# Graph-network kernel: part of the by-source sums moved from their own stage into the scatter stage

## The chip, the cores and the metric

One NeuronCore of one Trainium2 chip runs the whole kernel in one launch. The metric is device time in microseconds (us). The clock of TensorE that the throttle granted is recorded beside the instructions.

## The reference

There are 3125 nodes with 128 features and 53125 directed edges (`src`, `dst`, sorted by `dst`, self-loops included) with 128 features each. Four residual layers follow one another, each on `relu(layernorm(x))`:

```
h = relu(layernorm(x))
L0: agg = sum of edge_attr over edges by src + by dst;  x += relu([h, agg] @ W1 + b1) @ W2 + b2
L1: agg = sum of edge_attr over edges by dst;           x += relu([h, agg] @ W1 + b1) @ W2 + b2
L2: two graph convolutions with D^-1/2 A D^-1/2
L3: messages relu([h[src], h[dst], edge_attr] @ W) @ W2 + b, mean by dst, update MLP
```

The change concerns the sum of edge rows by `src` that L0 needs. Everything after the first two stages below stays as it is, but for small things named with the change.

## The kernel before

Edges come in 416 chunks of 128, two chunks make a pair (208 pairs), four chunks or two pairs make a group (104 groups). Nodes come in 25 blocks of 128.

**Scatter stage** (`place_and_count`, from 26 to 557 us). For each pair the engines do this. SyncE (SP) loads a group's edge rows into one of 8 buffers. VectorE (DVE) makes one-hots of the pair's blocks and of its window of 24 destinations (`hots`, L814 and L821). ScalarE (ACT) makes one-hots of the low part of the source (`lows`, L786 and L789) and copies the source key into the edge rows (`key_in_row`, L779). TensorE (PE) multiplies them into PSUM (L921 for a table of counts between nodes, L927 for the sums by destination, L930 for counts by destination). DVE adds the pair's result to the tables in SBUF (`collect`, L853 and L855); in the order of the code, `collect(i - 2)` comes behind `hots(i)`.

Once a group, PE computes ranks of the edges within their source blocks (`rank`, L901, L892, L905), DVE turns them into a row number of the table `rows_by_block` in DRAM (`own_rank` L834, `place` L839, `place_whole` L843), and GpSimd (POOL) writes the group's rows there with four indirect DMAs (L769). `which_block` (L828) makes the one-hots that a later `rank` needs; in group g it waits for `rank(g + 1)`, since they share two buffers. A `value_load` of the window's first column stands ahead of each `collect`. ACT copies the running counts to SBUF (`base_of_next`, L793).

The order on PE within a group g, with the even pair i = 2g and the odd pair i + 1, is: three matmuls of ones (L384, into a bank that nobody reads; 16 instead of 3 ahead of every 32nd pair), `rank(g + 1)`, the even pair, three matmuls of ones, the odd pair. The order on DVE is: even step: `place`, `hots`, `place_whole`, `which_block(g + 2)`, `collect`; odd step: `hots`, `collect`, `own_rank(g + 1)`.

**Sum stage** (`sum_blocks`, from 559 to 686 us). `rows_by_block` holds for each block of source nodes room for 18 tiles of 128 rows (9 for the last block). SP reads it in 74 reads of up to 6 tiles into 4 buffers, a read waiting for the sums of the fourth before it. DVE compares the keys with an iota (L1125), PE multiplies rows by the one-hots (L1181, a float32 product is recorded as two matmuls), and DVE adds the sum of each block to the sums by destination (L1117). Beside it DVE takes the statistics of x (L1068, L1147), and ACT checks 25 stripes of the table of counts for overflow (L1164). A short block with the flags and twelve matmuls of ones follows (L1201 to L1225), and then the dense layers.

Of the kernel before, what the change touches and what calls it, by code (L numbers as in the profile page):

```python
# [81 lines left out]
LAST_BANK = 7  # L82
WARM_EVERY = 32


class Signal:
# [6 lines left out]
    def __init__(self, make, everywhere=False):  # L93
        self.make, self.everywhere, self.on_path, self.base = make, everywhere, {}, {}

    @property
    def h(self):
        branch = Signal.path is not None and not self.everywhere
        if branch not in self.on_path:
            self.on_path[branch] = self.make()  # L100
        return self.on_path[branch]
# [44 lines left out]
def build(nc, x, src, dst, ea, l0, l1, l2, l3, out):  # L146
    ctx = ExitStack()
    with ctx:
# [7 lines left out]
        def signal(name, everywhere=False):  # L156
# [3 lines left out]
            return Signal(make, everywhere)  # L160
# [98 lines left out]
        bounds = sb("bounds", [1, 2, NB])  # L259
        over = sb("over", [1, 2, NB])  # L260
# [22 lines left out]
        tab_row = sb("tab_row", [1, 2, 2, ST * P], I32)  # L283
        tab_bc = sb("tab_bc", [P, 2, 2, ST * P])

        shifts = [sb(f"shift{k}", [P, SLOTS_OF[k], GS[k]]) for k in range(2)]
# [15 lines left out]
        junk = grid_space.take([P, NP], U8)  # L302
        excess = grid_space.take([P, NB])
# [349 lines left out]
        pair_done = signal("pair_done")  # L653
        taken = signal("taken")
# [68 lines left out]
        def place_and_count():  # L723
# [15 lines left out]
            with nc.Block(no_gpsimd_drain=True) as block:  # L739
                @on(block.sync)  # L740
                def _(sp):
                    for g in range(ROWG, GROUPS):
# [6 lines left out]
                        if g == 6 * ROWG:  # L749
                            sp.wait_ge(vec.h, vec.at(1))  # L750
                            sp.dma_start(x_nm[:, 0:NB - 1, :], x[0:(NB - 1) * P, :].rearrange("(b p) f -> p b f", p=P)).then_inc(loaded.h, 16)
                            sp.dma_start(x_nm[0:NLAST, NB - 1, :], x[(NB - 1) * P:N, :]).then_inc(loaded.h, 16)
                    sp.wait_ge(loaded.h, loaded.at(16 * 23))
# [19 lines left out]
                def _(act):  # L773
# [16 lines left out]

                    def base_of_next(g):
                        act.wait_ge(ranks_read.h, ranks_read.at(g + 1))
                        act.activation(bases[:, (g + 1) % 2, :], acc[0:1, R_AT + RANKS:R_AT + RANKS + NK], ACT.Copy).then_inc(based.h, 1)  # L793
# [4 lines left out]
                    for i in range(PAIRS):  # L798
# [4 lines left out]
                        if i % PG == 1 and g + 1 < GROUPS:  # L803
                            base_of_next(g + 1)

                @on(block.vector)
                def _(dve):
# [50 lines left out]

                    which_block(0)
                    which_block(1)  # L860
                    own_rank(0)
                    for i in range(PAIRS + 2):
# [9 lines left out]
                        if i >= 2:  # L872
                            collect(i - 2)
                        if i % PG == 1 and g + 1 < GROUPS:
                            own_rank(g + 1)
                        if i == 4 * ROWG * PG:
                            dve.wait_ge(tail_zero.h, tail_zero.at(32))
                            dve.memset(x_nm[:, NB - 1, :], 0.0).then_inc(vec.h, 1)
                    dve.memset(odd[:, 3:5], 0.0)
                    dve.tensor_scalar(bounds[:, 0, 0:NB - 1], iota[0:1, 0:NB - 1], float(CAP), float(FILLED), ALU.mult, ALU.add)  # L880
# [6 lines left out]
                    dve.tensor_tensor(over[:, 1, :], bases[:, GROUPS % 2, 0:NB], bounds[:, 1, :], ALU.is_gt)  # L887

                @on(block.tensor)
                def _(pe):  # L890
# [1827 lines left out]
```

## Time and profile before

| what | value |
|---|---|
| median of the runs shown | 1446.84 us (1445.10 to 1453.07, 3 runs) |
| the profiled execution, its own time | 1445.09 us |
| its span, first to last instruction | 1443.2 us |
| mean granted clock of TensorE | 0.971 of full |
| busy share PE / DVE / ACT / POOL | 86% / 61% / 38% / 56% |

A busy share is an average over stages. In a timeline row the first number is the start in us from the span's start, the second how long the row lasts, then engine, line, operation, and tiles as out<-in. Brackets give idle time of the engine ahead of the row and what ended it. A time of a matmul includes the way through the array, so the start of the next one tells better how long it holds the engine.

### The profile page before, as it was taken

What the parts mean: (1) busy time and instruction counts of PE and PEld (TensorE: products, weight loads), DVE (VectorE), ACT (ScalarE), POOL (GpSimd) and SP (SyncE); (2) the same over time, 40 slices, a digit from 0 to 9 for tenths busy, and PEclk for the clock granted to TensorE, in tenths of its full rate; (3) what the DMA queues carried; (4) which work ended last, traced back from release to release, by engine and by line L of the source; (5) the groups of instructions that cost most, each with busy time, mean ns of one, the idle gap of its engine ahead of it and who ended that gap; (6) DMA issues with size and microseconds to landing.
All of it is one profiled execution on the core that took longest, in us unless ns stands there. A gap on an engine that the chain in (4) does not pass through costs nothing. (4 is left out here: it accounts for less than half of the span.)

```text
span 1443.2 us, 32570 instructions
## 1 busy us (share of the span) xinstructions
PE 1243.0 (86%) x9643; PEld 908.2 (63%) x9644; DVE 881.1 (61%) x2785; ACT 555.4 (38%) x1465; POOL 809.5 (56%) x844
## 2 busy tenths in 40 slices
PE   5887888888888887898679998999999988898896
PEld 3554555555555555888459997477766766666665
DVE  6777878787877876766676537344444444444343
ACT  5444444444454446960222103333332222222222
POOL 5777777777777773000000000777777777777774
PEclk9999999999999999999889998899999999999997
DMA  7533335333333324877600001745555565555641
GB/s 230 137 106 104 104 105 148 102 105 104 106 104 106 107 72 138 237 246 217 30 18 2 2 1 52 203 133 153 156 154 155 161 159 150 152 140 145 149 111 42
DMA packets 198603, 174.73 MB, mean 121 GB/s; under 512 B 48820, under 2 KB 171174, under 8 KB 198342
## 3 DMA queue, kind: packets, MB, share of 16 engines
q1 hardware_dynamic: 171848, 118.36, 31.1%
q0 software_dynamic: 26624, 54.79, 12.9%
q8 instruction: 62, 1.02, 0.3%
q14 instruction: 69, 0.57, 0.2%
HBM read 134.89 MB, written 38.16 MB: 120 GB/s over the span
## 5 line engine op out<-in xcount | busy, mean ns | idle before, releaser
L2192 POOL DMA_INDIRECT between<-p_table,src_g x416 | 397.5, 956 | 472.5 <-DMA p_table<-n_nm 346.0
L384 PE MATMUL acc<-ones_b 128*128 128x512 bf16 x1603 | 425.5, 386 | 29.3 <-PEq L1407 15.5
L769 POOL DMA_INDIRECT rows_by_block<-h_t,mean_bc x312 | 300.6, 963 | 109.5 <-issue 77.1
L384 PEld LDWEIGHTS acc<-ones_b 128*128 128x128 bf16 x1603 | 142.5, 99 | 130.9 <-issue 39.2
L921 PE MATMUL acc<-n_nm 128*128 128x384 bf16 (+1 forms) x832 | 140.8, 291 | 87.2 <-DVE n_nm L821 86.4
L2302 ACT ACTIVATE between<-acc 128x256 f32<-128x256 f32 x208 | 79.9, 384 | 352.4 <-PE acc L2359 339.3
L853 DVE TENSOR_TENSOR between<-between,acc 128x600 f32 x208 | 161.3, 775 | 61.3 <-issue 51.7
L2391 PE MATMUL acc<-w_msg,between 128*128 128x128 f32 x832 | 184.1, 303 | 0.0
L2370 PEld LDWEIGHTS acc<-between 128*128 128x128 f32 x832 | 128.9, 197 | 71.4 <-issue 52.2
L2229 DVE TENSOR_TENSOR between<-acc,between 128x256 f32<-128x256 f32 x208 | 87.6, 421 | 139.9 <-DMA between<-p_table,src_g 90.0
L921 PEld LDWEIGHTS acc<-n_nm 128*128 128x128 bf16 x832 | 66.3, 97 | 164.0 <-DVE n_nm L821 134.8
L2370 PE MATMUL acc<-between 128*128 128x24 f32 x832 | 132.5, 240 | 42.4 <-DVE agg_sum L2269 40.7
L821 DVE TENSOR_SCALAR n_nm<-iota_w,agg_sum 128x600 bf16<-128x600 f16 x416 | 154.5, 412 | 0.0
L786 ACT ACTIVATE away<-iota_b,agg_sum 128x128 bf16<-128x128 bf16 x416 | 140.9, 385 | 0.0
L2391 PEld LDWEIGHTS acc<-w_msg,between 128*128 128x128 f32 x832 | 126.0, 191 | 1.7 <-issue 0.3
L793 ACT ACTIVATE bases<-acc 1x26 f32<-1x26 f32 x104 | 19.0, 182 | 265.7 <-DVE agg_sum L834 265.7
L1181 PE MATMUL acc<-n_nm,h_t 128*128 128x128 f32 x882 | 109.4, 280 | 11.5 <-DVE n_nm L1125 10.9
L769 POOL DMA_INDIRECT rows_by_block<-agg_sum,mean_bc x104 | 99.7, 959 | 32.5 <-issue 25.5
L2359 PE MATMUL acc<-ident,between 128*128 128x128 f32 x416 | 114.1, 275 | 0.0
L1181 PEld LDWEIGHTS acc<-n_nm,h_t 128*128 128x128 f32 x882 | 102.2, 191 | 18.8 <-DVE n_nm L1125 18.1
L789 ACT ACTIVATE n_nm<-away,ones 128x256 bf16<-128x256 bf16 x208 | 105.6, 508 | 6.8
L2269 DVE TENSOR_TENSOR agg_sum<-agg_sum,acc 128x24 f32 x208 | 37.4, 180 | 115.3 <-PE acc L2370 65.5
(204 smaller groups left out, 1950.4 us busy)
## 6 DMA issues: line engine op xcount, KB each, us to landing
h_t<-rows_by_block SPq DMA_DIRECT2D x73, 387.0 KB, 3.8
between<-in_edge_attr SPq DMA_DIRECT2D x207, 128.0 KB
h_t<-in_edge_attr SPq DMA_DIRECT2D x78, 256.0 KB, 3.2
between<-in_dst SPq DMA_DIRECT2D x51, 288.0 KB
between<-p_table,src_g POOLq DMA_INDIRECT x416
agg_sum<-in_edge_attr SPq DMA_DIRECT2D x25, 256.0 KB
rows_by_block<-h_t,mean_bc POOLq DMA_INDIRECT x312
rows_by_block<-x_nm SPq DMA_DIRECT2D x1, 4644.0 KB, 18.6
```

The lines of the kernel that those rows point to most:

```text
L384: pe.matmul(acc[:, bank * BANK:(bank + 1) * BANK].rearrange("p (a n) -> p a n", n=P), ones_b[:, :], ones_b[:, :].rearrange("p (a n) -> p a ...
L769: pool.indirect_dma_start(rows_by_block, bass.IndirectOffsetOnAxis(ap=place_in_table[:, t:t + 1], axis=0), row_group(g)[:, j, :], None).th ...
L786: act.activation(away[:, h + j, :], iota_b[:, :], ACT.Abs, scale=-1.0, bias=lo_s[:, 2 * i + j:2 * i + j + 1])\
L789: act.activation(low_hot[:, h:h + 2, :], away[:, h:h + 2, :], ACT.Relu, scale=-1.0, bias=ones[:, 0:1]).then_inc(lows_made.h, 1)
L821: ins = dve.tensor_scalar(wide_hot[:, i % HOTB * 2 + j, :], iota_w[:, :], key_w[:, t:t + 1], None, ALU.is_equal)
L853: dve.tensor_tensor(between[:, :, bass.ds(first, W)], between[:, :, bass.ds(first, W)], acc[:, o:o + NB * WS].rearrange("p (b w) -> p b w" ...
L921: pe.matmul(acc[:, to:to + (b1 - b0) * WS].rearrange("p (b w) -> p b w", w=WS)[:, :, 0:W], low_hot[:, h + j, :], wide_hot[:, h + j, b0 * W ...
L1181: last = pe.matmul(acc[:, o:o + P], rows_in_block[:, q, j, 0:D], hot_in_block[:, q, j, :], start=is_first and j == 0, stop=is_last and j = ...
L2192: pool.indirect_dma_start(got[:, q, j * D:(j + 1) * D], None, p_table, bass.IndirectOffsetOnAxis(ap=src_g[:, n * G + j:n * G + j + 1], axi ...
L2359: last = pe.transpose(acc[:, o:o + P], rows[:, i, j, :], ident[:, :])
L2370: last = pe.matmul(acc[:, o:o + W], relued[:, i % MR, j, :], onehot[:, i * G + j, :], start=j == 0, stop=j == G - 1)
L2391: last = pe.matmul(acc[:, o:o + P], turned[:, i % MR, j * P:(j + 1) * P], w_msg[:, 2, :], start=False, stop=True)
```

## The change

Seventy-two chunks of 384 rows of `rows_by_block`, that is the first nine tiles of each of the 24 full blocks, are summed within the scatter stage. SP loads chunk m in its step of group m + 32 (three buffers; it waits for the sum three chunks before). ACT makes the one-hots in group m + 29: three operations of Abs and one of Relu, both float32. PE sums the chunk in group m + 30, ahead of the odd pair, in place of the three matmuls of ones there: three float32 products into the one idle bank. DVE takes it out in group m + 31 into a new table `home`, behind `collect` of the odd step. As there is one bank, `sum_chunk(m)` waits for `take_chunk(m - 1)`. `rank` moves ahead of the ones of the even pair. The wait for `taken` moves ahead of the ones too, which now go to the pair's own bank. The 16 ones come ahead of an even pair.

In the sum stage each full block has nine tiles left, as reads of 6 and 3; 50 reads in all. The load of x moves from the scatter stage to behind the fifth read. ACT checks 14 stripes alone, and the other 11 as one that DVE unites with ten bitwise ors of 800 words (r = 5 to 14). DVE adds `agg_dst` to `home` once (3072 columns), statistics come two to a read from read 16 on. The 16 ones at its start become 6, the 12 ones of the flags' block go, and the first dense layer gets three. Three comparisons with bounds come at the end of the scatter stage, and some semaphores of the general path are shared with others.

```diff
+CT = 3
+CROWS = CT * P
+CRING, CHOTS = 3, 3
+CHUNK_LOAD, CHUNK_HOT, CHUNK_SUM, CHUNK_TAKE = 32, 29, 30, 31
+CHUNKS = EC // KC - CHUNK_LOAD
...
 @on(block.sync)
+                    def load_chunk(m):
+                        if m >= CRING:
+                            sp.wait_ge(chunk_summed.h, chunk_summed.at(m + 1 - CRING))
+                        row = m % (NB - 1) * CAP + m // (NB - 1) * CROWS
+                        sp.dma_start(chunk_rows[:, m % CRING, :, :], rows_by_block[row:row + CROWS, :].rearrange("(p j) w -> p j w", j=CT))\
+                          .then_inc(chunk_in[m % CRING].h, 16)
...
+                        if g >= CHUNK_LOAD:
+                            load_chunk(g - CHUNK_LOAD)
...
 @on(block.scalar)
+                    def hots_of_chunk(m):
+                        act.wait_ge(chunk_in[m % CRING].h, chunk_in[m % CRING].at(16 * (m // CRING + 1)))
+                        if m >= CHOTS:
+                            act.wait_ge(chunk_summed.h, chunk_summed.at(m + 1 - CHOTS))
+                        h = chunk_hot[:, m % CHOTS, :, :]
+                        for j in range(CT):
+                            act.activation(h[:, j, :], iota[:, :], ACT.Abs, scale=-1.0, bias=chunk_rows[:, m % CRING, j, D:KW]).then_inc(chunk_away.h, 1)
+                        act.wait_ge(chunk_away.h, chunk_away.at(CT * (m + 1)))
+                        act.activation(h, h, ACT.Relu, scale=-1.0, bias=ones[:, 0:1]).then_inc(chunk_hots.h, 1)
...
+                        if i % PG == 0 and 0 <= g - CHUNK_HOT < CHUNKS:
+                            hots_of_chunk(g - CHUNK_HOT)
...
 @on(block.vector)
+                    def take_chunk(m):
+                        dve.wait_ge(chunk_summed.h, chunk_summed.at(m + 1))
+                        at = home[:, m % (NB - 1) * P:m % (NB - 1) * P + P]
+                        o = IDLE_BANK * BANK
+                        if m < NB - 1:
+                            dve.tensor_copy(at, acc[:, o:o + P]).then_inc(chunk_taken.h, 1)
+                        else:
+                            dve.wait_ge(chunk_taken.h, chunk_taken.at(m + 2 - NB))
+                            dve.tensor_tensor(at, at, acc[:, o:o + P], ALU.add).then_inc(chunk_taken.h, 1)
...
                         if i >= 2:
                             collect(i - 2)
+                        if i % PG == 1 and 0 <= g - CHUNK_TAKE < CHUNKS:
+                            take_chunk(g - CHUNK_TAKE)
                         if i % PG == 1 and g + 1 < GROUPS:
                             own_rank(g + 1)
...
 @on(block.tensor)
+                    def sum_chunk(m):
+                        pe.wait_ge(chunk_hots.h, chunk_hots.at(m + 1))
+                        if m >= 1:
+                            pe.wait_ge(chunk_taken.h, chunk_taken.at(m))
+                        o = IDLE_BANK * BANK
+                        for j in range(CT):
+                            last = pe.matmul(acc[:, o:o + P], chunk_rows[:, m % CRING, j, 0:D], chunk_hot[:, m % CHOTS, j, :],
+                                             start=j == 0, stop=j == CT - 1)
+                        last.then_inc(chunk_summed.h, 1)
...
                     for i in range(PAIRS):
                         g, q, c = i // PG, i // PG % ROWG, i % PG * 2
-                        stream_ones(pe, IDLE_BANK, WARM_UP if i % WARM_EVERY == WARM_EVERY - 1 else WARM_PAIR)
                         if c == 0 and g + 1 < GROUPS:
                             rank(g + 1)
+                        if i >= PRING:
+                            pe.wait_ge(taken.h, taken.at(i + 1 - PRING))
+                        if c != 0 and 0 <= g - CHUNK_SUM < CHUNKS:
+                            sum_chunk(g - CHUNK_SUM)
+                        else:
+                            stream_ones(pe, at_bank(i) // BANK, WARM_UP if i % WARM_EVERY == WARM_EVERY - 2 else WARM_PAIR)
                         pe.wait_ge(hots_made.h, hots_made.at(i + 1))
                         pe.wait_ge(lows_made.h, lows_made.at(i + 1))
-                        if i >= PRING:
-                            pe.wait_ge(taken.h, taken.at(i + 1 - PRING))
...
 sum_blocks
-                for j in range(0, n, LR):
+                done = CT * sum(b < k for k in BY_CHUNK)
+                for j in range(done, n, LR):
...
+                        if r == LB_IN:
+                            sp.wait_ge(vec.h, vec.at(1))
+                            sp.dma_start(x_nm[:, 0:NB - 1, :], x[0:(NB - 1) * P, :].rearrange("(b p) f -> p b f", p=P)).then_inc(loaded.h, 16)
...
-                        dve.tensor_tensor(agg_sum[:, b * P:b * P + P], acc[:, o:o + P], agg_dst[:, b * P:b * P + P], ALU.add).then_inc(agg_read.h, 1)
+                        dve.tensor_tensor(agg_sum[:, b * P:b * P + P], acc[:, o:o + P], home[:, b * P:b * P + P], ALU.add).then_inc(agg_read.h, 1)
...
-                    stream_ones(pe, LAST_BANK, WARM_UP)
+                    stream_ones(pe, LAST_BANK, WARM_SHORT // 2)
```

## Rows read from the trace of the kernel before

**Rows 1.** The profile page, its first line.
```profile
span 1443.2 us, 32570 instructions
```

**Rows 2.** Windows over both stages: busy us of each engine, PEclk, DMA share, GB/s.
```profile
562.30:684.20 121.90, 110.58 (x884) 102.06 (x883) 80.92 (x147) 74.58 (x49) 0.00 (x0) 0.99 0.77 235
26.00:557.30 531.30, 439.81 (x3491) 273.49 (x3489) 416.17 (x1297) 253.75 (x824) 400.32 (x416) 1.00 0.37 106
```

**Rows 3.** Timeline of POOL, first DMAs of two groups.
```profile
305.25 0.96 POOL L769 DMA_INDIRECT rows_by_block<-agg_sum,mean_bc  x1 [0.30 <-ACT h_t L779]
...
310.30 0.96 POOL L769 DMA_INDIRECT rows_by_block<-agg_sum,mean_bc  x1 [0.30 <-ACT h_t L779]
```

**Rows 4.** Timeline of DVE over one group of the scatter stage.
```profile
304.00 0.65 DVE L821 TENSOR_SCALAR n_nm<-iota_w,agg_sum 128x600 bf16<-128x600 f16 x2
...
305.37 0.27 DVE L828 TENSOR_TENSOR agg_sum<-iota,agg_sum 128x104 bf16<-128x104 f32 x1 [0.46 <-PE acc L905]
306.19 0.78 DVE L853 TENSOR_TENSOR between<-between,acc 128x600 f32 x1 [0.55 <-issue]
...
307.00 0.87 DVE L821 TENSOR_SCALAR n_nm<-iota_w,agg_sum 128x600 bf16<-128x600 f16 x2
307.79 0.77 DVE L853 TENSOR_TENSOR between<-between,acc 128x600 f32 x1
...
308.59 0.25 DVE L834 TENSOR_TENSOR agg_sum<-acc,agg_sum 128x104 f32<-128x104 f32 x1
...
310.43 0.27 DVE L828 TENSOR_TENSOR agg_sum<-iota,agg_sum 128x104 bf16<-128x104 f32 x1 [0.24 <-PE acc L905]
```

**Rows 5.** Timeline of PE over the same group.
```profile
307.92 0.69 PE L921 MATMUL acc<-n_nm 128*128 128x384 bf16 x4 [0.95 <-DVE n_nm L821]
...
308.88 0.81 PE L384 MATMUL acc<-ones_b 128*128 128x512 bf16 x3
309.62 0.48 PE L901 MATMUL acc<-bases,ones 1*128 1x130 f32 x2
...
310.28 0.67 PE L921 MATMUL acc<-n_nm 128*128 128x384 bf16 x4
```

**Rows 6.** Groups of instructions by line: busy us, mean ns | idle before them.
```profile
L1125 DVE TENSOR_TENSOR n_nm<-iota,h_t 128x768 f32<-128x768 f32 x73 | 69.9, 957 | 40.4 <-DMA h_t<-rows_by_block 39.5
L1125 DVE TENSOR_TENSOR n_nm<-iota,h_t 128x384 f32<-128x384 f32 x1 | 0.6, 558 | 1.3 <-DMA h_t<-rows_by_block 1.3
L1117 DVE TENSOR_TENSOR agg_sum<-acc,by_dst 128x128 f32<-128x128 f32 x25 | 6.6, 269 | 0.0
L786 ACT ACTIVATE away<-iota_b,agg_sum 128x128 bf16<-128x128 bf16 x416 | 140.9, 385 | 0.0
```

**Rows 7.** Timeline of PE: the first sums, and the ones of the flags' block.
```profile
564.88 7.19 PE L1181 MATMUL acc<-n_nm,h_t 128*128 128x128 f32 x60
...
687.95 2.75 PE L384 MATMUL acc<-ones_b 128*128 128x512 bf16 x12
```

**Rows 8.** Windows in the message stage, columns as in rows 2.
```profile
1274.00:1280.00 6.00, 4.12 (x33) 3.04 (x32) 1.50 (x6) 1.13 (x4) 4.48 (x6) 1.00 0.73 170
1281.00:1283.00 2.00, 2.00 (x12) 1.82 (x11) 1.54 (x6) 0.26 (x1) 1.64 (x2) 0.50 0.48 140
...
1418.00:1424.00 6.00, 3.35 (x30) 2.84 (x28) 1.54 (x5) 1.76 (x5) 4.48 (x6) 0.99 0.27 77
...
1075.00:1081.00 6.00, 4.52 (x38) 3.40 (x36) 2.57 (x8) 1.38 (x5) 4.66 (x5) 1.00 0.53 153
```

**Rows 9.** Timeline of PE: pauses ahead of those windows, and four ones at either clock.
```profile
1278.87 0.37 PE L2370 MATMUL acc<-between 128*128 128x24 f32 x2 [1.88 <-DVE agg_sum L2269]
...
593.68 2.50 PE L1181 MATMUL acc<-n_nm,h_t 128*128 128x128 f32 x20 [1.70 <-DVE n_nm L1125]
...
1205.80 1.91 PE L384 MATMUL acc<-ones_b 128*128 128x512 bf16 x4
1209.31 1.03 PE L384 MATMUL acc<-ones_b 128*128 128x512 bf16 x4
```

More of the change, by code:

```diff
@@ L154, in build, with signal @@
         made_signals = [0]
-        def signal(name, everywhere=False):
+        def signal(name, twin=None, everywhere=False):
             def make():
@@ L258, in build @@
         bases = sb("bases", [1, 2, NK])
-        bounds = sb("bounds", [1, 2, NB])
-        over = sb("over", [1, 2, NB])
+        chunk_space = Space(x_nm[:, :, :].rearrange("p b f -> p (b f)")[:, (CAP - FILLED) // P * KW if FILLED else 6 * KW:], F32)
+        chunk_rows = chunk_space.take([P, CRING, CT, KW])
+        chunk_hot = chunk_space.take([P, CHOTS, CT, P])
+        bounds = chunk_space.take([1, 2 + len(BY_CHUNK), NB])
+        over = chunk_space.take([1, 2 + len(BY_CHUNK), NB])
+        counts_at = chunk_space.take([1, len(BY_CHUNK), NB])
         low_bound = sb("low_bound", [P, 1])
@@ L280, in build @@
         b1_row = sb("b1_row", [P, H2])
-        tab_row = sb("tab_row", [1, 2, 2, ST * P], I32)
-        tab_bc = sb("tab_bc", [P, 2, 2, ST * P])
-        shifts = [sb(f"shift{k}", [P, SLOTS_OF[k], GS[k]]) for k in range(2)]
+        home = sb("home", [P, NP])
+        general_space = Space(home[:, :], F32)
+        tab_row = general_space.take([1, 2, 2, ST * P], I32)
+        tab_bc = general_space.take([P, 2, 2, ST * P])
+        shifts = [general_space.take([P, SLOTS_OF[k], GS[k]]) for k in range(2)]
         win_f = sb("win_f", [1, PAIRS])
@@ L653, in build @@
         pair_done = signal("pair_done")
+        chunk_in = [signal(f"chunk_in{q}") for q in range(CRING)]
+        chunk_away = signal("chunk_away")
+        chunk_hots = signal("chunk_hots")
+        chunk_summed = signal("chunk_summed")
+        chunk_taken = signal("chunk_taken")
         taken = signal("taken")
@@ L887, in _ @@
                     dve.tensor_tensor(over[:, 1, :], bases[:, GROUPS % 2, 0:NB], bounds[:, 1, :], ALU.is_gt)
+                    for c, n in enumerate(BY_CHUNK):
+                        dve.tensor_tensor(over[:, 2 + c, 0:n], counts_at[:, c, 0:n], bounds[:, 2 + c, 0:n], ALU.is_lt)
                 @on(block.tensor)
@@ L941, in place_and_count @@
             away_made.passed(EC)
-            loaded.passed(16 * 23)
+            for s in (chunk_hots, chunk_summed, chunk_taken):
+                s.passed(CHUNKS)
+            chunk_away.passed(CT * CHUNKS)
+            for q in range(CRING):
+                chunk_in[q].passed(16 * len(range(q, CHUNKS, CRING)))
+            loaded.passed(16 * 21)
             vec.passed(2)
@@ L1162, in _ @@
                 def _(act):
-                    for b in range(NB):
-                        act.activation(junk[:, :], between[:, b, :], ACT.Relu, bias=low_bound[:, :], accum_out=excess[:, b:b + 1]).then_inc(checked.h, 1)
-                        if b < NB - 1:
+                    for b in range(ALONE + 1):
+                        if b == ALONE:
+                            act.wait_ge(united.h, united.at(NB - ALONE - 1))
+                        of = between[:, b, :] if b < ALONE else mean_bc[:, 2 * EC:2 * EC + NP // 4].bitcast(U8)
+                        act.activation(junk[:, :], of, ACT.Relu, bias=low_bound[:, :], accum_out=excess[:, b:b + 1]).then_inc(checked.h, 1)
+                        if b < ALONE:
                             act.wait_ge(checked.h, checked.at(b + 1))
@@ L1188, in sum_blocks @@
             agg_read.passed(NB)
-            checked.passed(NB)
+            homes.passed(1)
+            far_read.passed(1)
+            loaded.passed(32)
+            checked.passed(ALONE + 1)
+            united.passed(NB - ALONE - 1)
             vec.passed(4)
```

93 lines of the change are left out of this document (61 added, 32 removed).

## The prediction

> **What bounds the kernel now.** I read the page's span, then windows over the two stages, then one group of the scatter stage on each engine in the timeline, then groups by line. The scatter stage is 531 of 1443 us; no engine fills it: PE is busy 440 us, DVE 416, POOL 400, at full clock throughout [rows 1, 2]. POOL issues its four DMAs of a group in 5.06 us without a pause beyond 0.30 [rows 3]. DVE's group takes the same 5.06 us, from one `which_block` (L828) to the next [rows 4].
>
> That match hides a second bound, a circle between DVE and PE, which the rows show as starts that hang on each other: L828 at 305.37, the even `collect` 306.19, odd `hots` 307.00 to 307.87, the odd pair on PE 307.92, ones 308.88, `rank` 309.62, L828 again 310.43 [rows 4, 5]. L828 waits for `rank`, `rank` stands behind the odd pair in PE's order, and the odd pair waits for `hots`. There is no slack in it but what POOL adds: two L821 in a row take 0.65 us beside no hold-up and 0.87 us in the odd step [rows 4], so the circle alone would take some 4.84 us and is held at POOL's pace.
>
> The sum stage is bound by its reads: 441 tiles of 66 KB (128 x 129 x 4 bytes) are 29.1 MB in 121.9 us, while DVE is busy 81 us and waits 40 us for reads [rows 2, 6]. PE is nearly full there, 111 us [rows 2].
>
> **Scatter stage, groups with a chunk.** The sums go where ones stood, and DVE's operation is short, but the place decides. `sum_chunk(m)` runs in group m + 30 ahead of the odd pair, and waits for `take_chunk(m - 1)`. That one runs in group (m - 1) + 31, the same group, on DVE behind the odd `collect`. So the odd pair, which waited for odd `hots` alone, now waits for `collect`, the take and the sum as well. Behind it on PE stand `rank` and, through it, L828. The new circle, from L828:
> - to where a take can start, that is where L834 starts now: 308.59 - 305.37 = 3.22 us, less 0.22 us where POOL does not hold the two L821: 3.00 [rows 4];
> - the take, like L1117 (128x128 out of PSUM): 0.27 us [rows 6]; 0.05 us to PE (307.87 to 307.92 now);
> - the sum: three float32 products are six recorded matmuls, 7.19 / 60 = 0.12 us each [rows 7]: 0.72 us;
> - the odd pair, 308.88 - 307.92 = 0.96 us; then `rank`: 310.43 - 309.62 = 0.81 us and 0.10 us ahead of it. The ones between (0.64 us) are gone from here, since `rank` moved ahead of them [rows 5].
>
> Sum: 3.00 + 0.27 + 0.05 + 0.72 + 0.96 + 0.91 = 5.91 us. I take 5.95, for a rest of POOL's hold-ups; ends 5.85 and 6.15 (all of the 0.22 stays). Against 5.06 that is 0.89 us more in 71 groups (31 to 101; the first sum waits for no take): **+63 us** at full clock.
>
> The clock may not stay. In the new circle PE does ones and the even pair until 1.6 us past L828 (0.64 + 0.96), and then waits until 3.3: a pause of 1.7 us in every 5.95 us. It is busy 4.25 us of 5.95, 72%; today its pause is 0.95 us [rows 5]. In the message stage a pause of 1.88 us, in six microseconds with PE busy 4.12, was followed by the lower of the two levels, 1.2 instead of 2.4 GHz; another fall followed six microseconds at 3.35. None followed six at 4.52, nor the single pause of 1.70 us in the sum stage [rows 8, 9]. Six microseconds of the new circle have 4.3, close to the first case; and here the pause returns each time, beside pairs whose L927 and L930 stream only 24 columns. I take it that the clock falls again and again. At half clock four ones take 1.91 us instead of 1.03 [rows 9], a doubling of what lies between starts; PE's 0.72 + 0.96 + 0.81 double, so the circle is 5.95 + 2.4 = 8.3 us. In that state PE has hardly a pause left, so the clock should come back, as it came back between 1205.8 and 1209.3 us, with PE at work throughout [rows 9]. With a third of the time at half clock the mean is 1 / (0.667 / 5.95 + 0.333 / 8.3) = 6.57 us: 1.51 x 71 = **+107 us**. A fifth of the time gives 6.31 (+89), three quarters 7.56 (+177).
>
> The Trainium skill (TensorE: Matmul & The Clock Gate, HAM oscillation) describes loops whose matmuls wait in every step and which fall to the lower clock in each; by it the state would recur as I take it, and this trace shows only single falls.
>
> **Groups without a chunk** (1 to 29). With `rank` ahead of the ones the circle is 4.84 - 0.64 = 4.2 us, and DVE's own work some 4.3. POOL still needs 5.06, but has eight buffers to fall behind in, and DVE's lead is kept as the later circle is slower than POOL. What DVE can gain is bounded by 0.75 x 29 = 22 us, and by nothing if POOL holds its L821 and casts at its own pace, as it does now. I take 0.3 us each, **-9 us**.
>
> For the low end there is a rule: The Trainium skill (SBUF — State Buffer, Who interferes with whom) calls the port pair of DVE and GpSimd an exclusive lock, in which the second to start waits for the whole instruction. By it this term would be near 0. The stretched L821 [rows 4] agrees in kind, but the stretch is 0.22 us, less than a DMA of 0.96.
>
> **Covered parts.** ACT: three Abs at no more than 0.385 [rows 6] and a Relu, about 1.6 us a group ahead of the odd `lows`, on an engine busy 254 of 531 us [rows 2]; those lows end some 1.7 us past L828, PE wants them at 4.0. SP: the chunk's load is issued after a sum, two circles ahead of ACT's need, some 7 us, and its wait delays the next group's load to five groups ahead of its use: nothing. 14 MB more traffic at a DMA share of 0.37: nothing. If a load lands late, ACT holds the odd pair; about 2 us of slack go first. POOL now waits for DVE, so its last group ends sooner: -1. The 16 ones move to where PE has its pause: nothing.
>
> **Sum stage.** 225 tiles are left, 14.9 MB, and x adds 1.6: at 235 GB/s 70 us. DVE: 80.9 - 70.5 + 25 x 0.957 + 25 x 0.558 + ten unions of 800 words (0.957 x 800 / 768 = 1.0 each) + 3072 columns of `home` (0.957 x 4 = 3.8) = 62 us. PE: 450 x 0.12 = 54 us. With three engines this close, six ones instead of 16 at a cold start, and x in the way of reads, I take 74 us instead of 122: **-48**, ends -52 and -40. ACT has 14 checks instead of 25 and ends earlier than that. Flags' block: the ones (2.75 us) ended it: **-2**, ends -3 and 0, since a colder clock follows.
>
> **Sum.** The profiled execution took 1445.1 us, 1.7 below the median of the runs. Fixed terms: -9 - 1 - 48 - 2 = -60. With the falling clock 1445.1 - 60 + 107 = 1492; against the median **1494 us**. Its own range, by 89 and 177, is 1475 to 1564.
>
> **The rivals.**
> 1. The clock holds. Then +63 meets -60: 1445.1 + 3 + 1.7 = 1450. By the ends (+56, -22, -52, -3, -3 against +77, 0, -40, 0, 0) 1423 to 1484. For: single pauses of 1.7 us passed, and 75% busy passed [rows 8, 9].
> 2. Faster: the circle isn't one, since POOL sets the pace. It has this for it that DVE idles over 1 us in each group and PE 0.95 [rows 4, 5], room for a take of 0.27 and 0.08 more on PE. The scatter stage stays at its length: 1446.8 - 1 - 48 - 2 = 1396. It decides from the point where the take could reach PE without delaying `rank` by over 0.2 us; the orders written in the code speak against it.
> 3. At half clock for most of the 71 groups: 3.2 x 71 = 230, 1617. Against it: full work brings the clock back.
>
> **Chances.** Forecast with a falling clock 0.60, rival 3 0.04, rival 1 0.24, rival 2 0.12. A change under 0.5% (7 us) can't be told from none in this kernel. Rival 1 lies on both sides: faster 0.06, within 0.5% 0.10, slower 0.08. So faster 0.18, same 0.10, slower 0.72. The range of 8 in 10 leaves out rival 2, rival 3 and the lowest part of rival 1: 1432 to 1565.
>
> **What would show it.** Scatter stage: L828 to L828 near 5.9 us or more from group 31 on, PE idle 1.7 us ahead of the sum, ended by DVE's take; POOL pausing for L843; PEclk below 1.00 in windows there. Before group 31, periods under 5.06. The reads of the sum stage within 70 to 82 us. Wrong, if the period with chunks stays near 5.06, if PE's sum waits for nothing, or if the clock stays at 1.00 (then 1450).

## The result, and the profile after

The changed kernel takes **1515.84 us** (median of 4 runs, 1509.24 to 1525.08); the kernel before, run beside it, 1446.32 (4 runs, 1445.1 to 1453.07). The ratio is 1.0493, with an interval of 1.0463 to 1.0522: slower. The profiled execution took 1509.24 us. On four of the five occasions on which the experiments below ran (e1 to e7, e11 and e12), every kernel, the one before too, took about 1,800 to 1,880 us, with stops of some 3 to 9 us in which DVE waits for nothing that the profile names, so from those runs only the groups without a stop, called quiet, are read, and their times and ratios (which leave out each kernel's slowest runs) decide nothing.

The page's first line and the clock's row of the changed kernel, in 40 slices of the span:

```profile
span 1507.4 us, 32653 instructions
...
PEclk9999878878887788689999999779999999999996
```

Windows over the changed kernel: groups 1 to 26 or so, groups 33 to 101, the sum stage (columns: length; busy us of PE, PEld, DVE, ACT, POOL; PEclk, DMA share, GB/s):

```profile
26.00:158.00 132.00, 121.72 (x970) 82.79 (x969) 108.04 (x357) 70.75 (x232) 99.97 (x104) 0.99 0.41 114
170.70:649.70 479.00, 390.71 (x2576) 291.67 (x2574) 282.09 (x943) 275.89 (x840) 281.57 (x292) 0.79 0.38 107
672.30:754.60 82.30, 61.27 (x450) 55.96 (x450) 60.26 (x144) 43.20 (x31) 0.00 (x0) 0.94 0.64 191
```

These answer to [rows 1, 2]. The clock, 1.00 through the whole scatter stage before, is 0.79 in the groups with a chunk and stays at 0.99 in those without. The sum stage moves 191 GB/s instead of 235, the rate in rows 2.

How long a group takes is read from the starts of `which_block` (L828 before, L870 after; one a group, two groups ahead). First the kernel before, then the changed one: the start that opens group 1, the one that ends group 29, the one that opens group 31, the last.

```profile
25.15 0.27 DVE L828 TENSOR_TENSOR agg_sum<-iota,agg_sum 128x104 bf16<-128x104 f32 x1
...
172.18 0.27 DVE L828 TENSOR_TENSOR agg_sum<-iota,agg_sum 128x104 bf16<-128x104 f32 x1 [0.37 <-PE acc L905]
177.04 0.27 DVE L828 TENSOR_TENSOR agg_sum<-iota,agg_sum 128x104 bf16<-128x104 f32 x1 [0.18 <-PE acc L905]
...
541.31 0.27 DVE L828 TENSOR_TENSOR agg_sum<-iota,agg_sum 128x104 bf16<-128x104 f32 x1 [0.46 <-PE acc L905]
```

```profile
25.63 0.27 DVE L870 TENSOR_TENSOR agg_sum<-iota,agg_sum 128x104 bf16<-128x104 f32 x1
...
158.17 0.27 DVE L870 TENSOR_TENSOR agg_sum<-iota,agg_sum 128x104 bf16<-128x104 f32 x1
163.34 0.27 DVE L870 TENSOR_TENSOR agg_sum<-iota,agg_sum 128x104 bf16<-128x104 f32 x1 [0.68 <-PE acc L964]
...
649.71 0.27 DVE L870 TENSOR_TENSOR agg_sum<-iota,agg_sum 128x104 bf16<-128x104 f32 x1 [1.44 <-PE acc L964]
```

So groups 1 to 29 went from 147.03 us to 132.54, **-14.5**, and groups 31 to 101 from 364.27 to 486.37, **+122.1**: 5.13 against 6.85 us a group. Five of these 71 groups hold the sixteen ones: at full clock they take 6.74 us before and 6.78 after, and the others mostly 5.05 and 6.00. Fourteen groups before took 4.82 to 4.86, which is the circle alone, 4.84, of the prediction. What DVE waits for ahead of that line, over the whole kernel (us, times), before and after:

```profile
  PE acc L905: 47.2, 99
```

```profile
  PE acc L964: 164.6, 84
```

That is 117 us more of waiting for `rank`. The rest of the span: the first one-hot of the sum stage to the last add went from 123.8 us (562.3 to 686.1) to 82.3 (672.3 to 754.6), **-41.5**; from there to the first dense center 5.5 to 3.1, **-2.4**; between the last `which_block` and the first one-hot 21.0 to 22.6, +1.6; start +0.5; all behind the sums 751.6 to 749.7, -1.9. With group 30 (+0.3) these make +64.2 us, the difference of the spans (1507.4 - 1443.2).

Now one group of the changed kernel, PE and then DVE. It begins at half clock and ends at full clock:

```profile
301.94 1.40 PE L972 MATMUL acc<-x_nm 128*128 128x128 f32 x6 [1.88 <-DVE home L906]
303.13 1.21 PE L993 MATMUL acc<-n_nm 128*128 128x384 bf16 x4
...
309.73 0.91 PE L972 MATMUL acc<-x_nm 128*128 128x128 f32 x6 [0.50 <-DVE home L906]
310.47 0.67 PE L993 MATMUL acc<-n_nm 128*128 128x384 bf16 x4
...
311.49 0.48 PE L960 MATMUL acc<-bases,ones 1*128 1x130 f32 x2
...
315.72 1.52 PE L972 MATMUL acc<-x_nm 128*128 128x128 f32 x6 [1.88 <-DVE home L906]
```

```profile
306.28 0.27 DVE L870 TENSOR_TENSOR agg_sum<-iota,agg_sum 128x104 bf16<-128x104 f32 x1 [3.18 <-PE acc L964]
...
308.50 0.77 DVE L895 TENSOR_TENSOR between<-between,acc 128x600 f32 x1
...
309.31 0.27 DVE L906 COPY home<-acc 128x128 f32<-128x128 f32 x1
...
312.31 0.27 DVE L870 TENSOR_TENSOR agg_sum<-iota,agg_sum 128x104 bf16<-128x104 f32 x1 [1.34 <-PE acc L964]
```

The circle can be walked in these rows. `which_block` 306.28, take 309.31 (3.03), sum 309.73 (0.42), odd pair 310.47 (0.74), `rank` 311.49 (1.02), `which_block` 312.31 (0.82): 6.03 us, of which the forecast had 3.00, 0.32, 0.72, 0.96 and 0.91. PE waits 0.5 to 1.9 us ahead of the sum for DVE's take, and DVE waits 1.3 to 3.3 us for PE's `rank`. In 66 of the 72 sums the sum starts 0.42 or 0.43 us after a take has started. Of the 71 groups, twelve with the usual three ones ran the whole circle at full clock, in 5.99 to 6.04 us, and five ran at half clock throughout, in 7.97 to 8.14. In between the clock goes to and fro, as in these two windows, which follow each other, of the changed kernel:

```profile
200.60:206.60 6.00, 4.11 (x38) 3.27 (x37) 4.32 (x16) 3.95 (x13) 4.50 (x5) 1.00 0.46 130
206.70:213.40 6.70, 6.70 (x34) 4.82 (x33) 3.09 (x9) 3.63 (x11) 5.18 (x6) 0.50 0.52 129
```

At full clock PE is busy 4.1 us in 6.0, and then the clock falls; at half clock it is busy without a break, and then comes back. In groups 31 to 101 the clock is at its lower level for 0.41 of the time.

### The profile page after: what moved, and what is told of

Same layout as the page of the kernel before. It is cut to its first block and busy times, and to the rows that moved or that the text cites. A ratio compares the mean times of both kernels' runs of the same rounds, so it can differ in the third digit from the quotient of the medians.

```text
span 1507.4 us, 32653 instructions
## 1 busy us (share of the span) xinstructions
PE 1285.3 (85%) x9408; PEld 976.7 (65%) x9409; DVE 854.6 (57%) x2852; ACT 632.3 (42%) x1736; POOL 810.4 (54%) x844
## 3 DMA queue, kind: packets, MB, share of 16 engines
q8 instruction: 62, 1.02, 0.3%
## 5 line engine op out<-in xcount | busy, mean ns | idle before, releaser
L398 PE MATMUL acc<-ones_b 128*128 128x512 bf16 x1368 | 387.1, 408 | 30.3 <-PEq L1517 13.1
L398 PEld LDWEIGHTS acc<-ones_b 128*128 128x128 bf16 x1368 | 131.4, 102 | 128.8 <-issue 44.3
L993 PE MATMUL acc<-n_nm 128*128 128x384 bf16 (+1 forms) x832 | 171.5, 338 | 1.3 <-ACT n_nm L816 1.3
L972 PE MATMUL acc<-x_nm 128*128 128x128 f32 x432 | 80.3, 334 | 90.7 <-DVE home L909 61.8
L993 PEld LDWEIGHTS acc<-n_nm 128*128 128x128 bf16 x832 | 93.4, 113 | 85.6 <-issue 41.3
L863 DVE TENSOR_SCALAR n_nm<-iota_w,agg_sum 128x600 bf16<-128x600 f16 x416 | 144.0, 388 | 0.0
L972 PEld LDWEIGHTS acc<-x_nm 128*128 128x128 f32 x432 | 65.6, 227 | 95.5 <-DVE by_dst L897 95.5
L870 DVE TENSOR_TENSOR agg_sum<-iota,agg_sum 128x104 bf16<-128x104 f32 x104 | 27.7, 267 | 169.3 <-PE acc L964 164.6
```

The lines of the kernel that those rows point to most:

```text
L398: pe.matmul(acc[:, bank * BANK:(bank + 1) * BANK].rearrange("p (a n) -> p a n", n=P), ones_b[:, :], ones_b[:, :].rearrange("p (a n) -> p a ...
L863: ins = dve.tensor_scalar(wide_hot[:, i % HOTB * 2 + j, :], iota_w[:, :], key_w[:, t:t + 1], None, ALU.is_equal)
L972: last = pe.matmul(acc[:, o:o + P], chunk_rows[:, m % CRING, j, 0:D], chunk_hot[:, m % CHOTS, j, :], start=j == 0, stop=j == CT - 1)
L993: pe.matmul(acc[:, to:to + (b1 - b0) * WS].rearrange("p (b w) -> p b w", w=WS)[:, :, 0:W], low_hot[:, h + j, :], wide_hot[:, h + j, b0 * W ...
```

## The experiments

Left to tell apart: how much of the 122 us is the wait itself and how much the clock; whether the place of the take makes the wait; what the order of `rank` and ones alone does; and why the sum stage brought less than forecast. All diffs but one are against the changed kernel.

### The take moved to the even step

```diff
-                        if i % PG == 1 and 0 <= g - CHUNK_TAKE < CHUNKS:
+                        if i % PG == 0 and 0 <= g - CHUNK_TAKE < CHUNKS:
```

Label e1_take_even:

> The changed kernel with one edit: DVE takes the chunk out in the even step of the same group instead of the odd one, behind the even collect. All work stays. Theory (the circle of DVE and PE through the wait for the take sets the stage): the take is then done some 1.9 us past which_block, the sum runs in PE's pause, and the circle is 0.27 (take) + 2.26 + 0.05 + 0.96 + 0.91 = about 4.5 us, under POOL's 5.06. The period of groups 31 to 101 falls from 6.85 to 5.06, the clock stays at its upper level in the scatter stage, and the time falls by 1.79 x 71 = 127 us, to about 1390. Rival A (the added work as such fills DVE or PE): the period stays above 5.5 and the time above 1430. Rival B (chunk loads or ACT's one-hots are late): period stays above 5.5 as well, with PE waiting for ACT.

Measured: 1860.03 us, with the kernel before at 1860.45 (ratio 1.0039, 0.9997 to 1.0081). The 1390 that was expected can't be tested here. The quiet groups from 31 on took down to 4.61 us at full clock, and mostly 6.60 to 6.61 at half clock: the circle of 6.0 is gone. The clock still was at its lower level for 0.41 of the time, beside the stops, so the run doesn't say what the clock would do without them.

The same kernel again, on three other chips:

> The kernel of e1_take_even once more, since in the four runs so far every kernel, the one before too, was some 400 us slower than in the runs that the result rests on. Theory of the circle: beside a kernel before at 1446, period 5.06 in groups 31 to 101, the clock up, about 1390. Rivals (the added work as such, or late chunks): period above 5.5, above 1430.

1858.95 us against 1858.93 (0.9986, 0.9923 to 1.0048); quiet groups down to 4.62.

> The take in the even step once more, for its time where the kernel before runs at about 1446 us. Theory of the circle: the circle's own time is 4.6 us (its shortest periods in the two runs so far), POOL's is 5.06, so POOL sets the period; the clock stays up, and the time is near 1390. Rival (something of the added work counts once the stage is not disturbed): above 1430. If the kernel before takes 1860 again, neither is told apart by the time, and the periods are read as before.

1863.76 against 1859.07 (1.0018, 0.9974 to 1.0063); quiet groups down to 4.74.

> The take in the even step, all else as in the changed kernel, for its time beside a kernel before at about 1450 us. Theory: as e8_reads_of_three without its gain of 13 us in the sum stage (69 us there against 82), so 1399, a ratio of 0.963; periods 4.7 to 4.8 undisturbed with a mean of 5.1 held by POOL's buffers, clock up in the scatter stage. Rival (a good part of the 136 us between the changed kernel and e8 came with the reads of three): above 1420.

1822.41 against 1839.23 (0.9866, 0.9773 to 0.9958), where 1399 and 0.963 were expected. The timeline of this last one, PE first, shows two quiet groups and then a stop:

```profile
303.03 0.91 PE L972 MATMUL acc<-x_nm 128*128 128x128 f32 x6 [0.51 <-issue]
...
307.74 0.91 PE L972 MATMUL acc<-x_nm 128*128 128x128 f32 x6 [0.50 <-ACT x_nm L826]
...
310.37 0.21 PE L964 MATMUL acc<-agg_sum,lower_b 128*128 128x104 bf16 x1
...
311.96 0.20 PE L1002 MATMUL acc<-agg_sum,ones_b 128*128 128x24 bf16 x2
318.62 1.62 PE L972 MATMUL acc<-x_nm 128*128 128x128 f32 x6 [6.47 <-DVE home L906]
```

```profile
316.57 0.27 DVE L870 TENSOR_TENSOR agg_sum<-iota,agg_sum 128x104 bf16<-128x104 f32 x1 [6.31 <-remote]
```

From sum to sum 4.71 us. Then DVE's `which_block`, whose `rank` had ended on PE at 310.58, starts only at 316.57, and PE waits for DVE. That is such a stop. Its cause is not in the trace.

### Ones in the pause

```diff
                         if c != 0 and 0 <= g - CHUNK_SUM < CHUNKS:
+                            stream_ones(pe, at_bank(i) // BANK, 7)
                             sum_chunk(g - CHUNK_SUM)
```

Seven ones ahead of each sum fill PE's pause; the wait for the take stays where it is. Label e2_ones_in_pause, and the same kernel later as e12_ones_in_pause, on the chip of e11:

> The changed kernel with seven more matmuls of ones ahead of each chunk's sum (7 x 0.21 = 1.5 us in the pause of 1.7 us); the wait for the take stays where it is. Theory (the pause lets the clock fall, and the fall adds to the wait): the clock stays at its upper level, every period of groups 31 to 101 is 6.0 us, as the undisturbed ones of the changed kernel are, and the time falls by 0.85 x 71 = 60 us to about 1456, still slower than before by under 1%. Rival (the long periods of 7.7 to 8.1 us come from something else, a late DMA or the port): the mean stays at 6.85 and the time at 1516 or above.

> The changed kernel with seven ones in PE's pause ahead of the sum, beside a kernel before at about 1450 us. Theory: the wait stays, the clock no longer falls; periods of groups 31 to 101 all near 6.0 us instead of a mean of 6.85 to 6.96, 60 to 68 us less than the changed kernel's 1522: 1454 to 1462, within 1% of the kernel before. Rival (the long periods have another cause): mean 6.8 or more, 1515 or above.

Measured: 1879.12 against 1860.45 (1.0093, 1.0054 to 1.0133), and 1800.95 against 1839.23 (0.9787, 0.9716 to 0.9857); the expected 1454 to 1462 can't be tested by these. The groups can be read. PE in the second run, and DVE's take ahead of the first of these sums:

```profile
310.47 1.68 PE L398 MATMUL acc<-ones_b 128*128 128x512 bf16 x7 [0.25 <-issue]
312.13 0.91 PE L972 MATMUL acc<-x_nm 128*128 128x128 f32 x6
...
316.47 1.69 PE L398 MATMUL acc<-ones_b 128*128 128x512 bf16 x7 [0.23 <-issue]
318.13 0.91 PE L972 MATMUL acc<-x_nm 128*128 128x128 f32 x6
```

```profile
311.70 0.28 DVE L906 COPY home<-acc 128x128 f32<-128x128 f32 x1
```

and a window over two of its groups, then one over two quiet groups of e11:

```profile
308.70:320.70 12.00, 11.53 (x87) 7.74 (x86) 7.90 (x27) 6.47 (x22) 6.67 (x8) 1.00 0.36 106
```

```profile
300.10:312.10 12.00, 10.79 (x95) 8.22 (x94) 8.15 (x27) 8.62 (x27) 7.72 (x9) 1.00 0.57 158
```

With the pause filled a quiet group takes the same 6.00 us from sum to sum, PE now busy 11.5 of 12 us. That leaves PE hardly idle, so one could take PE's own work for the new limit; but the sum still starts 0.43 us behind the start of the take (311.70 to 312.13), and 0.42 or 0.43 in 60 of the 72, as in the changed kernel. Of the 71 groups, 64 ran at full clock throughout (in e2 45), none wholly at half clock; the share of time at half clock was 0.05 (0.18 in e2), though the stops were there, instead of 0.41. So the 6.00 is the wait for the take, and the clock no longer falls time and again once the pause is filled. Whether it is the length of the pause or PE's busy share that counts, these runs don't separate, as both change. An estimate for the changed kernel: at full clock throughout, 66 groups at 6.00 and five at 6.78 make 6.05 on average, so (6.05 - 5.13) x 71 = 65 us are the wait, and the other (6.85 - 6.05) x 71 = 57 us the clock.

### The sum moved to the even pair

```diff
-CHUNK_LOAD, CHUNK_HOT, CHUNK_SUM, CHUNK_TAKE = 32, 29, 30, 31
+CHUNK_LOAD, CHUNK_HOT, CHUNK_SUM, CHUNK_TAKE = 32, 29, 30, 30
...
-                        if c != 0 and 0 <= g - CHUNK_SUM < CHUNKS:
+                        if c == 0 and 0 <= g - CHUNK_SUM < CHUNKS:
...
-                            stream_ones(... WARM_UP if i % WARM_EVERY == WARM_EVERY - 2 else WARM_PAIR)
+                            stream_ones(... WARM_UP if i % WARM_EVERY == WARM_EVERY - 1 else WARM_PAIR)
```

Label e3_sum_even_pair, and the same kernel as e7_sum_after_pair:

> The changed kernel with the chunk's sum in the place of the ones of the even pair, the ones back ahead of the odd pair (16 of them every 16 groups), and the take in the odd step of the same group as the sum. All work stays. Theory of the circle: the sum stands off the circle, in the time in which PE waits for the odd one-hots, and needs no take of its own group; the take needs a sum that is done 1.5 us past which_block. Period 5.06 (POOL's), the clock up, time about 1390, within 0.5% of the variant that takes in the even step. Rival (any sum in the group costs its 0.72 us on PE): period 5.7, time about 1435.

> The chunk's sum in the place of the ones of the even pair, once more beside the kernel above. Theory: the circle's own time is 4.6 us here as well, POOL's 5.06 decides, and the time is within 0.5% of the kernel above. Rival (a sum on PE always costs its 0.7 us): 5.7 us a group, 45 us more than the kernel above.

Measured: 1847.32 against 1860.45 (0.999, 0.9933 to 1.0048), and 1852.43 against 1859.07 (0.9973, 0.9937 to 1.0009). Quiet groups took down to 4.58 and 4.59 us at full clock and from 6.15 at half clock. So the circle of 6.0 also goes when the sum is moved instead of the take, and the rival, 5.7 us a group for any sum on PE, is out. Whether this order is better or worse than the even take, these runs can't say.

### The order alone, without chunks

Against the kernel before:

```diff
-                        stream_ones(pe, IDLE_BANK, WARM_UP if i % WARM_EVERY == WARM_EVERY - 1 else WARM_PAIR)
                         if c == 0 and g + 1 < GROUPS:
                             rank(g + 1)
+                        stream_ones(pe, IDLE_BANK, WARM_UP if i % WARM_EVERY == WARM_EVERY - 2 else WARM_PAIR)
```

Label e4_order_alone:

> The kernel before with one edit: rank ahead of the ones of the even pair (the 16 ones go ahead of an even pair as well); no chunks. Theory: the circle shortens from 4.84 to 4.2 us, but POOL's four DMAs take 5.06 us a group, so DVE's lead grows by 0.5 us a group only until the eight row buffers are used up, and the stage ends with POOL: the time stays within 0.5% of before, at 1440 to 1447, with the 16 ones no longer costing a part of 1.7 us each. Rival (the lead of the first 29 groups was a real gain of that edit): 15 to 50 us less, 1430 or below.

Measured: 1866.56 against 1860.45 (1.0077, 1.004 to 1.0115), where a time within 0.5% of before was expected. Groups 1 to 29 took 6.97 us on average, the quickest of all groups 4.39. The run shows that DVE can go at 4.4 without chunks, and is inconclusive on what the order brings over a whole stage.

### Three on one chip: the change, the take first, the take even with shorter reads

Here the kernel before took 1452.65 us (7 runs). The changed kernel unedited, label e9_changed_again:

> The changed kernel itself, unedited, beside the kernel before in the state in which that takes 1860 us, to tell what the other runs of this state are to be compared with. Theory (the circle costs 6.0 us at the upper clock, 8.1 at the lower, and the take in the even step 4.6 and 6.6): undisturbed periods at the same values as in the profile after, and a scatter stage 60 to 110 us longer than with the take in the even step, so 1920 to 1970. Rival (where other waits of this state rule, the circle hides behind them): within 20 us of the variant that takes in the even step, 1860 to 1880.

Measured: **1521.83 us** (1.0485, 1.0448 to 1.0522), as the first time. Its expectation, 1920 to 1970, was for a chip on which the kernel before takes 1860, and isn't tested by this. Groups 1 to 29 took 4.56 us, groups 31 to 101 6.96, at half clock 0.47 of the time; the usual full-clock group again 6.00.

The take ahead of one `collect`, still in the odd step, label e10_take_first:

```diff
-                        if i >= 2:
-                            collect(i - 2)
                         if i % PG == 1 and 0 <= g - CHUNK_TAKE < CHUNKS:
                             take_chunk(g - CHUNK_TAKE)
+                        if i >= 2:
+                            collect(i - 2)
```

> The changed kernel with the take in the odd step ahead of the odd collect instead of behind it. The circle loses one collect (853 and 855 of the kernel before: 0.69 + 0.11 = 0.80 us) between the one-hots and the take. Theory: undisturbed periods of groups 31 to 101 of 6.00 - 0.80 = 5.2 us at the upper clock and 8.06 - 0.80 = 7.26 at the lower. Rival (PE's sum or the port, not DVE's order, sets the 6.0): 6.0 stays.

Measured: **1411.44 us** (0.9717, 0.9676 to 0.9758). Of the 71 groups, 52 took 5.18 to 5.20, and the five with sixteen ones 6.78. PE ahead of two sums, and a window over its groups with a chunk:

```profile
301.79 0.91 PE L972 MATMUL acc<-x_nm 128*128 128x128 f32 x6 [1.08 <-DVE home L909]
...
307.22 0.91 PE L972 MATMUL acc<-x_nm 128*128 128x128 f32 x6 [1.32 <-DVE home L909]
```

```profile
171.00:560.00 389.00, 314.19 (x2671) 243.59 (x2669) 300.52 (x995) 282.97 (x859) 297.25 (x302) 0.99 0.47 134
```

One swap of two operations on DVE, whose `collect` takes 0.81 us from its start to the next operation's (309.31 - 308.50), cuts the period by 0.81 as expected, PE's pause from 1.88 to 1.1 to 1.3, and the half-clock share from 0.47 to 0.02. PE still waits for the take ahead of 64 of the 72 sums: the circle is there, only shorter. Against e9 the groups 31 to 101 take (6.96 - 5.34) x 71 = 115 us less, and the whole kernel 110. This is the one pair of runs that changes nothing but the place of the take, side by side on one chip.

The take in the even step, and in the sum stage reads of three tiles into eight buffers instead of six into four, label e8_reads_of_three (with eight buffers the same line of code puts the load of x behind the ninth read instead of the fifth, and the statistics start at read 32):

```diff
-LR = 6
-LB_IN = 4
+LR = 3
+LB_IN = 8
...
-                        if i % PG == 1 and 0 <= g - CHUNK_TAKE < CHUNKS:
+                        if i % PG == 0 and 0 <= g - CHUNK_TAKE < CHUNKS:
```

> The variant that takes in the even step, with reads of three tiles in eight buffers in the sum stage instead of six in four (75 reads, up to 24 tiles under way instead of some 18; the statistics start at read 32 instead of 16). Theory: the sum stage of the changed kernel takes 82 us from its first one-hot to its last add instead of the 74 of my forecast, because SP waits 56 us for sums that free a buffer, so the ring sets the rate; with the deeper ring it takes 74 to 76. Rival (the load of x and the lower clock at the stage's start cost the eight us): it stays at 81 to 83. The scatter stage is as without this edit.

Measured: **1385.97 us** (0.9542, 0.9501 to 0.9583): it beats both kernels. Its windows over groups 33 to 101 and the sum stage:

```profile
170.00:527.00 357.00, 317.40 (x2586) 239.86 (x2585) 284.32 (x947) 278.04 (x842) 271.24 (x282) 0.97 0.49 142
560.40:629.30 68.90, 58.71 (x451) 53.89 (x450) 61.71 (x171) 45.02 (x33) 0.00 (x0) 0.97 0.82 235
```

A group takes 4.77 us at the median, 5.10 on average, with 0.06 of the time at half clock. The circle isn't gone here either: PE waits for the take ahead of 61 of the 72 sums, by some 0.5 us. But from `which_block` through the even take, the sum, the odd pair and `rank` it takes as little as 4.61 us, less than the 5.04 of POOL's four DMAs, and the average, 5.10, is near that. The sum stage takes 68.9 us at 235 GB/s, less than the 74 to 76 expected, where e9 and e10, with reads of six, take 85.3 and 84.8. What SP waited for in that stage (us, times, longest), in the kernel before, the changed kernel and this one:

```profile
SPq L1106 <- PE acc L1181: 94.5, 69, 5.4
```

```profile
SPq L1190 <- PE acc L1288: 55.7, 42, 4.8
```

```profile
SPq L1190 <- PE acc L1288: 31.6, 57, 2.5
```

SP's waiting by itself tells little: it is longest in the kernel before, which reads at 235 GB/s. The stretch behind x's load, with about the same work left in both (381 and 389 matmuls of PE), tells more; the changed kernel, then this one:

```profile
692.00:754.60 62.60, 48.68 (x381) 44.17 (x379) 47.35 (x129) 23.70 (x19) 0.00 (x0) 1.00 0.65 191
```

```profile
576.00:629.30 53.30, 48.00 (x389) 44.64 (x387) 47.36 (x149) 29.58 (x23) 0.00 (x0) 1.00 0.78 218
```

So some 9 of the 13.4 us between the two stages come behind x's load, at full clock in both, and the rest around it.

Against e9 the 135.9 us of span come from the scatter stage to its last `which_block` (130.8 less), POOL, which is now behind and has to catch up (10.6 more to the first one-hot), the sum stage (16.4 less) and 0.7 more elsewhere. The take in the even step with reads of six has no time beside a kernel before at 1450, so its share is known from this split and not from a run of its own.

## Why the prediction was right, step by step

**Right: the side, the range and the mechanism.** 1515.84 lies in 1432 to 1565 and 22 us above the 1494. The new circle exists, and it is the one walked in the forecast: a take that stands too late on DVE, in front of a sum that stands ahead of the odd pair and `rank` on PE. e10 shows that the place of the take makes it, since one `collect` less ahead of it gives back the time of that `collect` in every group; e1, e3 and e8 show that the 6.0 goes when either end is moved; what is left with the even take is a shorter circle, 4.6 us, that POOL's pace covers.

The 22 us come from terms of both signs. From profile to profile the change was +64 instead of +47: 15 us more in groups 31 to 101, 6.5 more in the sum stage, 2.6 more between the two stages, 5.5 less in groups 1 to 29, and some 1.5 less in small ones. The other 5 us are that the profiled execution was the quickest of its four, 6.6 us under their median.

**The circle at full clock**: forecast 5.95, measured 6.00. The two terms that were off cancel nearly: from the take to the sum 0.42 us, not 0.32 (a take out of PSUM and the step to PE), and 0.82 for `rank` and its wait, not 0.91. Where the take could start, the sum and the odd pair stood within 0.06.

**The clock**: that it would fall again and again was right, by the reading of pauses in [rows 8, 9]: the granted clock goes to 0.50 and back 25 times in these groups, where before it stayed at 1.00, and e10, e2 and e12 show that it hardly does so once the pause is shorter or filled. The Trainium skill (TensorE: Matmul & The Clock Gate, HAM oscillation) describes a loop that waits for a DMA in every step and falls to the lower clock in every one; the trace agrees in kind, though here the wait is for DVE and 25 falls in 71 groups are fewer than one a step. Its size is the term that was mis-sized, and the third of the time was a choice that no row gave. Forecast were a third and 8.3 us, measured are 0.41 (0.47 in e9) and 8.0: by the forecast's own formula 1 / (0.59 / 6.00 + 0.41 / 8.0) = 6.69. The measured mean is 6.85. Of the further 0.16, at least 0.05 are the five groups with sixteen ones, 0.78 us longer each, which the forecast put at nothing (before, they were 1.69 longer than the others); the rest lies in groups in which the clock changes, of which the longest with three ones took 8.23 us. In all +122 instead of +107. At half clock the circle grew by 2.0 and not by 2.4 us: in the group behind the timelines above the sum went from 0.74 to 1.31 us and the odd pair from 1.02 to 1.90, but `rank` with the step to DVE only from 0.82 to 1.25, not 1.6. (The 72% busy of the forecast is 71%, 4.25 of 5.95.)

**Groups 1 to 29**: forecast -9, measured -14.5. DVE gained 0.50 us a group, not 0.30, and POOL did not hold it. One pair of L863 and two starts of `which_block` there (the next is 158.17, above) and, beside them, POOL's DMAs:

```profile
146.32 0.86 DVE L863 TENSOR_SCALAR n_nm<-iota_w,agg_sum 128x600 bf16<-128x600 f16 x2
...
149.31 0.27 DVE L870 TENSOR_TENSOR agg_sum<-iota,agg_sum 128x104 bf16<-128x104 f32 x1
...
153.78 0.27 DVE L870 TENSOR_TENSOR agg_sum<-iota,agg_sum 128x104 bf16<-128x104 f32 x1
```

```profile
149.62 0.96 POOL L796 DMA_INDIRECT rows_by_block<-h_t,mean_bc  x1 [0.30 <-ACT h_t L806]
...
154.66 0.96 POOL L796 DMA_INDIRECT rows_by_block<-h_t,mean_bc  x1 [0.30 <-issue]
```

DVE goes at 4.4 us while POOL goes on at 5.04 (149.62 to 154.66, three of its DMAs between). POOL fell 17 us further behind by group 30 and had caught up by group 42. So the end of the range in which POOL holds DVE is out. The pair of L863 takes 0.66 us at the median in these groups and over 0.80 in three of 59, where before it was 0.76 and 19 of 60; the 0.86 above is a stretch of 0.2 us, not of a whole DMA of 0.96. The rule of the port pair as an exclusive lock (the Trainium skill, SBUF — State Buffer, Who interferes with whom), by which this term would have been near 0, is thus not borne out as a limit of the pace here; whether a shorter hold of the pair is behind the stretch, no run shows.

**The sum stage**: forecast -48 (74 us, ends 70 and 82), measured -41.5 (82.3 us, of 123.8 to the last add), at the weak end. The step that failed took the reads' rate over from before. Each block's nine tiles are now a read of six and one of three, and a read of three holds one of the four buffers as a read of six does, so that some 18 tiles are under way instead of 24, and the rate falls to 191 GB/s. Added to this is what x costs SP:

```profile
675.96 0.86 SPq L1193 DMA_DIRECT2D x_nm<-in_x  x1
676.86 3.80 SPq L1194 DMA_DIRECT2D x_nm<-in_x  x1
...
686.39 0.56 DVE L1213 TENSOR_TENSOR n_nm<-iota,h_t 128x384 f32<-128x384 f32 x1 [6.71 <-DMA h_t<-rows_by_block]
```

SP issues x for 4.7 us, no read of rows beside it, and DVE then idles 6.7 us for the next. e8, with reads of three in eight buffers and 24 tiles under way, has the rate of before and 68.9 us. It issues the same x load, and there DVE has buffers in hand and no such idle time. By the windows under e8 the ring of buffers is the larger part, some 9 of the 13 us, behind x's load; an edit of the ring or of x alone was not run.

**The small terms**: the flags' block -2.4 (forecast -2). "POOL ends sooner, -1" did not come: the way from the last `which_block` to the first one-hot is 1.6 us longer. ACT, SP's queue and the added traffic cost nothing in the groups: by the page of the changed kernel (line; busy us, mean ns | idle before, releaser), PE's idle time ahead of the sum is ended by DVE's takes (L909 61.8 of the 90.7 us, and L906 most of the rest), not by ACT.

```profile
L972 PE MATMUL acc<-x_nm 128*128 128x128 f32 x432 | 80.3, 334 | 90.7 <-DVE home L909 61.8
```

**The rivals.** That the clock holds is out by the row PEclk and 0.79. That POOL sets the pace is out for the change as made, though its arithmetic (1396) is near what the kernel gives once the circle is shortened: 1411 with the take first, 1386 with the even take and the shorter reads. That the clock would stay low for most of the time didn't happen: the share is 0.41 to 0.47.

## What to carry to other kernels

When work is put into an engine's idle time, look which wait comes with it and what stands behind that wait in the same engine's order; if it leads back to the engine that is waited for, the two engines make a circle, and its length is the sum of the steps in it, however idle both are. One swap of two neighbours on DVE was worth 110 us here. Work that is taken out of a place in which PE then pauses also has to be counted with the clock: nearly half of what the groups with a chunk lost was PE at half clock, by the estimate above, and filler belongs where the pause is, not where the old filler stood. A ring of buffers was worth its bytes here and not its count, so if the pieces get smaller, try more of them.

## What the runs showed of the hardware

- A pause of 1.9 us in every 6.0, with PE busy 4.1, let the clock fall 25 times within 71 groups; a pause of 1.1 to 1.3 in 5.19 (e10) hardly ever (0.02 of the time), and one of 0.25 in 6.00 (e12) hardly either (0.05; 0.18 in e2).
- POOL's indirect DMAs and DVE's operations in step, as before the change (5.06 and 5.05 us a group), were no sign of a shared limit: once `rank` came earlier, DVE went at 4.4 us beside POOL's 5.04.
- SP issued the load of x, 1.6 MB in two pieces, for 0.86 and 3.80 us, with no other read issued meanwhile.
- DVE can stand idle for 6.31 us (e11) at an operation whose producer on PE had ended 5.99 us before it started. What makes such stops stays open.
